# State-space turn: exponential of the decays in two halves, and both diagonal additions ahead of the sum of the squares of C

## What is computed

```python
Bm = rope(rmsnorm((x @ WB.T).reshape(B_, L, H, N), Bn_w) + B_bias, theta_cumsum)
Cm = rope(rmsnorm((x @ WC.T).reshape(B_, L, H, N), Cn_w) + C_bias, theta_cumsum)
alpha = exp(dt * A); beta = (1 - lam) * dt * alpha; gamma = lam * dt
h_t = alpha_t * h_(t-1) + beta_t * B_(t-1) x_(t-1) + gamma_t * B_t x_t
y_t = C_t h_t          # H = 64 heads, N = 128, L = 512 steps
```

## Time and profile before

| | |
|---|---|
| median of three executions | 5811.55 us (5810.41 to 5811.68) |
| profiled execution, own time | 5810.73 us |
| its span in the trace | 5808.9 us |
| busy over the span: TensorE matmul / weight load | 90% / 64% |
| busy over the span: VectorE / ScalarE / GpSimd | 77% / 59% / 63% |
| the decays' exponential (line 1546), first and last start | 1332.0 and 5086.8 us, 257 of them |

### The profile page before, as it was taken

How to read it: one execution, slowest core, us unless ns; L and a number is a source line. 1 busy time by engine, 2 the same in 40 slices (tenths; PEclk the granted TensorE clock), 3 DMA queues, 4 the chain that set the end, 5 groups by cost and what they waited for, 6 DMA issues and landing times. The chain is left out here.

```text
span 5808.9 us, 126387 instructions
## 1 busy us (share of the span) xinstructions
PE 5209.8 (90%) x38740; PEld 3727.2 (64%) x38997; DVE 4462.6 (77%) x6792; ACT 3440.1 (59%) x4750; POOL 3637.6 (63%) x4101
## 2 busy tenths in 40 slices
PE   5899679659999999999999999999999999973799
PEld 3444357546666676667666666666666677662687
DVE  5777555547888888888888888888888888825344
ACT  2444322136777777777777777777777777711222
POOL 2222100018999999999999999999999999900100
PEclk8888679879999999999999999999999999986899
DMA  2333300131111111111111111111111111131100
GB/s 96 108 111 112 95 33 29 47 125 35 36 35 35 34 35 36 33 36 33 36 33 35 32 38 34 35 33 36 33 35 33 35 36 33 32 118 55 37 18 18
DMA packets 452683, 275.46 MB, mean 47 GB/s; under 512 B 270648, under 2 KB 381976, under 8 KB 451640
## 3 DMA queue, kind: packets, MB, share of 16 engines
q1 hardware_dynamic: 434872, 264.57, 16.5%
q10 hardware_dynamic: 17664, 9.44, 0.6%
HBM read 194.15 MB, written 66.85 MB: 45 GB/s over the span
## 5 line engine op out<-in xcount | busy, mean ns | idle before, releaser
L1556 ACT ACTIVATE ss_r<-ss_pssum,ss_eps 128x512 f32<-128x512 f32 x256 | 176.8, 691 | 647.9 <-PE ss_pssum L1482 647.9
L1459 PE MATMUL ss_psse<-ss_rot 64*128 64x128 f32 x8224 | 528.2, 278 | 1.3 <-ACT ss_dec L1546 1.3
L1395 POOL TENSOR_TENSOR ss_own<-ident,ss_tk 128x512 f32<-128x512 f32 x512 | 524.9, 1048 | 0.0
L1459 PEld LDWEIGHTS ss_psse<-ss_rot 64*128 64x128 f32 x8224 | 479.1, 188 | 44.6 <-issue 43.2
L48 PE MATMUL ss_psc<-x_hi,ss_whi 128*128 x1024 | 505.0, 493 | 0.0
L1351 POOL TENSOR_TENSOR ss_dec<-ss_dec,ss_own 128x512 f32<-128x512 f32 x257 | 328.2, 1277 | 205.9 <-ACT ss_dec L1546 205.9
L48 PE MATMUL ss_psb<-x_hi,ss_whi 128*128 x1024 | 424.7, 415 | 30.7 <-issue 19.1
L1620 DVE SCALAR_TENSOR_TENSOR ss_psc<-ss_psc,ss_norm,ss_r 128x512 f32<-128x512 f32 x512 | 387.2, 756 | 77.1 <-ACT ss_r L1558 77.1
L1657 DVE TENSOR_TENSOR ss_gm<-ss_psse,ss_dec 128x1024 f32<-128x1024 f32 x257 | 314.7, 1225 | 131.5 <-POOL ss_dec L1355 131.5
L50 PE MATMUL ss_psc<-x_hi,ss_wlo 128*128 x1024 | 403.0, 394 | 0.0
L50 PE MATMUL ss_psb<-x_hi,ss_wlo 128*128 x1024 | 401.8, 392 | 0.0
(11 more groups left out here) (346 smaller groups left out, 15491.7 us busy)
## 6 DMA issues: line engine op xcount, KB each, us to landing
ss_dtb<-time_steps SPq DMA_DIRECT2D x516, 128.0 KB, 2.9
ss_wraw<-in_w_state SPq DMA_DIRECT2D x264, 80.0 KB, 2.3
ss_grown<-growths SPq DMA_DIRECT2D x1028, 8.0 KB
head_rows<-a_yhi SPq DMA_DIRECT2D x64, 256.0 KB, 2.4
a_qs<-head_rows SPq DMA_DIRECT2D x128, 96.0 KB, 2.2
a_ks<-head_rows SPq DMA_DIRECT2D x128, 96.0 KB, 2.2
ss_xp<-x_heads SPq DMA_DIRECT2D x33, 256.0 KB, 4.3
y_heads<-ss_yo SPq DMA_DIRECT2D x132, 64.0 KB, 2.4
```

The source lines that it names most:

```text
L1395: last = G.tensor_tensor(own[:, h * TPB:(h + 1) * TPB], g.ident[:].rearrange("p (o t) -> p o t", o=1).broadcast_to([P, TPB, P]), at_diagon ...
L1459: last = M(p_se[:, h * TPB + c, :], rot[at, 1 - j, e, cols], rot[at, 1 - j, 2 + e, cols], start=e == 0, stop=e == 1)
```

## The change

ScalarE makes the exponential of the decays in two instructions of 128x512, each with an increment of `d_done`, which so counts two per turn. GpSimd first adds both halves of the diagonal, each behind its half of the exponential, gives `dd_done`, and only then waits for `sq_c` and adds the squares of C. TensorE's `scores` waits for the second count. Nothing else differs.

```diff
--- before.py
+++ after.py
@@ -1346,13 +1346,15 @@
                 G.tensor_tensor(rot[:, 1 - j, 3], rot[:, 1 - j, 3], tmp[:, 1, 1], ALU.add).then_inc(rot_c, 1)
 
             def decays(k, squares_c):
-                pool.wait_ge(d_done, k + 1)
                 pool.wait_ge(own_done, k)
-                G.tensor_tensor(dec[:, 0:TPB], dec[:, 0:TPB], own[:, 0:TPB], ALU.add)
+                for h in range(2):
+                    pool.wait_ge(d_done, 2 * k + h + 1)
+                    half = slice(h * TPB, (h + 1) * TPB)
+                    last = G.tensor_tensor(dec[:, half], dec[:, half], own[:, half], ALU.add)
+                last.then_inc(dd_done, 1)
                 if squares_c:
                     pool.wait_ge(sq_c, k + 1)
                     G.tensor_tensor(sq[:, 1, 0], sq[:, 1, 0], sq[:, 1, 1], ALU.add).then_inc(ss_c, 1)
-                G.tensor_tensor(dec[:, TPB:2 * TPB], dec[:, TPB:2 * TPB], own[:, TPB:2 * TPB], ALU.add).then_inc(dd_done, 1)
 
             with pool.Fori(0, UNITS // 2) as n:
                 for j in range(2):
@@ -1450,7 +1452,7 @@
 
             def scores(k, j):
                 pe.wait_ge(rot_c, k + 1)
-                pe.wait_ge(d_done, k + 1)
+                pe.wait_ge(d_done, 2 * k + 2)
                 for c in range(TPB):
                     cols = slice(c * P, (c + 1) * P)
                     for e in range(2):
@@ -1543,7 +1545,8 @@
 
             def decays(k):
                 act.wait_ge(e_done, k + 1)
-                A(dec[:], p_se[:], ACT.Exp).then_inc(d_done, 1)
+                for h in range(2):
+                    A(dec[:, h * TPB:(h + 1) * TPB], p_se[:, h * TPB:(h + 1) * TPB], ACT.Exp).then_inc(d_done, 1)
 
             def take_b(k, j, e):
                 act.wait_ge(turned[e], k + 1)
```

## The result

The changed kernel takes 5849.85 us in the median (5845.43 to 5850.04), the kernel before 5810.98 us on the same chip (5809.65 to 5811.68): a ratio of 1.0063, 95% interval 1.005 to 1.0075. The forecast said slower, by 65 us; it is slower by 39 us. In the profiles the span grows from 5808.9 to 5843.6 us, and all of it lies in the state-space stage. From the first exponential of the decays to the last turn's it took 3754.8 us before; now it takes 5120.2 - 1329.1 = 3791.1, so 36 us more.

What follows compares the result with a forecast made beforehand. The prediction took a loop through several engines, meeting at TensorE's squares of C, as the bound. Lateness of 0.255 us in 256 turns gave 65 us, so 5877 us on the 5811.55 median, range 5840 to 5920.

Steps and rivals of the forecast that it cites:

- The path: TensorE's sum of the squares of C, with 0.28 us to spare, is made late by GpSimd's sum and lengthens every turn.
- The terms up to squares C: Exponential start to TensorE's squares of C: 0.60 half, 0.08 handoff, two 1.23 adds, 1.27 squares, 0.12 handoff, 4.53 us.
- The line from 384 to 1024 columns: Estimate of ScalarE's half exponential from PSUM copies of 490 and 1010 ns: 594 ns for 512 columns.
- the page's 570: Trainium skill's estimate for ScalarE from PSUM, 172 cycles plus one a column at 1.2 GHz: 570 ns for 512 columns.
- The exponential's second half: On ScalarE it ends at 1.13 instead of 1.01 us; the 0.12 is hidden by the wait for the projection of C.
- The diagonal on VectorE: The mask multiply starts half a microsecond sooner and 131.5 us of waits vanish, but the norm of C is awaited: worth nothing.
- Both ways back begin only after squares C in TensorE's queue: Returns to the squares of B, by ScalarE's norm and VectorE or TensorE's own queue, both follow the squares of C; 7.87 us.
- the term 0.255 x 256: Lateness of TensorE's squares of C, 0.255 us, counted in full in all 256 turns: 65 us.
- a partial gain: Part of the lateness made up by a shorter first half of ScalarE's exponential; the range reaches down to 5840 us for it.
- No change: Squares of C on TensorE not late, as the first half lands sooner or the handoff hides in idle; 5812 us, chance 0.10.
- faster: VectorE's wait for the second diagonal closes the loop, 5680 us, or GpSimd is the bound, 5635 us; together chance 0.06.
- slower by more: The 0.40 us from GpSimd's end to TensorE's squares of C is all handoff, so 0.54 us counts: 138 us, 5950, chance 0.05.

Runs made afterwards that it cites:

- halves_only: The kernel before with the exponential in two halves and GpSimd's order left as it was; 5817.86 us against 5816.03, ratio 1.0004.
- after_dd_late: The changed kernel with `dd_done` given by GpSimd's second small product, behind the squares of C; ratio to the kernel before 1.0064.
- before_u8: The kernel before with TensorE's inner loop written out, eight turns in a body instead of two; 5861.25 us, ratio 1.0075.

## Why the prediction was right, and where it was off

- **The path.** Squares C as the point that every turn waits for, and GpSimd's sum as what makes it late: right. The new wait is in the trace, 0.26 us beyond the usual 0.20, as written.
- **The terms up to squares C.** The half took 587 ns in the median, 585 in the mean (0.60 taken), the adds 1.24 apart (1.23), the handoff from GpSimd 0.13 (0.12), together 4.54 against 4.53 us. The line from 384 to 1024 columns was 7 ns over the median, counting 594; the page's 570 was 17 under, so the row was the better guide.
- **The exponential's second half.** ScalarE's wait for the projection of C fell to 0.44 us, not 0.37: the pair takes 1.07 us instead of 1.13. It is hidden, as said, and `halves_only` shows it alone at 1.0004.
- **The diagonal on VectorE.** Worth nothing, as said; the wait for the norm of C grew to 1.11 us (1.07 forecast), and `after_dd_late` moved it back with no effect.
- **The step that failed** is "Both ways back begin only after squares C in TensorE's queue", and with it the term 0.255 x 256. There is a third way: chunk sums, VectorE's sums, the branch in TensorE's sequencer, the projection of B and what is queued behind it. It begins ahead of squares C and was the longest in every second turn. That made 0.234 us of the lateness free in 128 turns, 30 us of the sum. What remained is 36 us in the profile and 39 in the medians. The turn became 14.81 us, not 14.92.
- **What was luck.** 39 us lie below the 46 to 108 that the bounds of the terms gave. The result is inside the range only because that was stretched down to 5840 for a partial gain, from a first half that lands sooner. The half landed as forecast; the gain came from the branch, which no rival and no bound had.
- **What I passed over.** Only one way back was followed, and it happened to be one without a branch. In the other kind the trace of before has 0.67 us of idle ahead of the projection of B, put down to "issue". The numbers of the prediction pointed at it: the turn that I followed took 14.56 us and the mean is 14.67, so the other kind had to take 14.78, with 0.22 us that the path I followed does not have.
- **The rivals.** No change, faster and slower by more are all out: squares C are late, the waits of VectorE and GpSimd were not the bound, though GpSimd had the highest occupancy beside the matmuls (now 132.53 of 146 us), and the handoff is 0.13, not 0.40.

Not settled: why the shortest way back is 7.78 us in one kind of turn and 7.87 in the other. It is not the branch, since `before_u8` has 7.78 in the same turns without one. The traces show the place: VectorE's state step (line 1641) starts 0.67 us after the first 1620 ahead of it in these turns and 0.76 us in the others. No run asked for the cause.

## What to carry to other kernels

Removing waits that are followed by another wait on the same engine only moves idle time; look for the one instruction at which all ways round the loop meet, and ask whether the new order makes it late. When you price a delay there, list every chain that leads round it, the sequencer's own branch among them, and look at every kind of iteration: one that doesn't go through the delayed point hides as much of the delay as it was longer by. A loop's branch placed right behind a wait can lengthen every round that takes it (here by 8.090 - 7.785 = 0.31 us); put it where the engine still has work queued, and don't pay for it with a body so long that its code must be fetched again.

## What the runs showed of the hardware that I had not expected

- A loop's branch on TensorE, behind a wait: 0.93 us from the end of VectorE's sums to the next body's first weight load (the compare and branch 211 ns, the register work after it 203 ns), where the queue has nothing else to hide it; 0.55 us where no branch stands between.
- Doubling the body from two turns to four, or to eight, brings 5 to 6 us in the mean at each of 15 outer branches (the branch itself 3.6 and 3.8 us in the median instead of 0.21), with 3.01 and 5.10 MB of instructions loaded instead of 0.49.
- A 128x512 exponential from PSUM takes 587 ns in the median, one of 128x1024 1008 ns. By a line through these two points, an estimate, 166 ns are fixed and 0.822 ns go to a column.
